# A gated recurrence with its r and z gates in PSUM banks of their own: r's newest term and the whole of z as one fp32 matmul each

## What is computed

```python
def step(h, xs):
    xzt, xrt, xht = xs
    z = jax.nn.sigmoid(xzt + h @ U_z + vz)
    r = jax.nn.sigmoid(xrt + h @ U_r + vr)
    hh = jnp.tanh(xht + r * h @ U + vh)
    h_new = (1.0 - z) * h + z * hh
    return (h_new, h_new)
```

## Time and profile before

| | |
|---|---|
| median of 3 runs | 760.3 us (759.01 to 761.73) |
| span of the profiled execution | 755.7 us; its own time is not given apart from the span |
| recurrence in the span | 203.9 to 740.8 us |
| TensorE products busy | 640.4 us (85%) |
| TensorE weight loads busy | 528.5 us (70%) |
| VectorE, ScalarE, GpSimd busy | 461.1, 324.6, 178.0 us |
| granted TensorE clock, mean | 0.956 |

### The profile page before, as it was taken

One profiled execution on the slowest core, in us unless ns is written; L12 is line 12 of the kernel. 1 busy time (PEld: TensorE's weight loads), 2 busy tenths in 40 slices (PEclk: granted clock), 3 DMA queues, 4 the chain that ended last, 5 costly groups with the idle time before them and its releaser, 6 DMA issues.

```text
span 755.7 us, 26078 instructions
## 1 busy us (share of the span) xinstructions
PE 640.4 (85%) x7909; PEld 528.5 (70%) x7909; DVE 461.1 (61%) x3362; ACT 324.6 (43%) x1253; POOL 178.0 (24%) x789
## 2 busy tenths in 40 slices
PE   5998677656788888988889898889888889999995
PEld 4445566545677877877778787778777667877774
DVE  1536344343267777777777777777767556777663
ACT  2356434434145546455555555464544222322321
POOL 1023222221033232232232332322311001111110
PEclk9999967899589999999999999999999999999997
DMA  8022222222212221222212221212210000000000
GB/s 221 9 85 76 85 88 79 92 79 79 76 40 67 74 69 65 67 71 68 71 64 65 74 64 65 74 64 67 72 62 3 2 2 2 10 6 3 4 6 8
DMA packets 43965, 43.06 MB, mean 57 GB/s; under 512 B 5500, under 2 KB 43656, under 8 KB 43784
## 3 DMA queue, kind: packets, MB, share of 16 engines
q1 hardware_dynamic: 43328, 40.75, 16.6%
q10 hardware_dynamic: 584, 1.64, 0.6%
HBM read 20.95 MB, written 21.43 MB: 56 GB/s over the span
## 4 chain that ended last, share of the span: by engine, by line
PE 54%; DVE 14%; DMA 14%; issue 9%; ACT 7%; SPq 1%; DVEq 1%; ACTq 0%; POOLq 0%; POOL 0%
DMA skew<-e_sb 13%; PE bank L622 12%; PE bank L635 12%; PE bank L423 7%; PE bank L407 6%; DVE s_sb L845 3%; ACT hh L765 3%; PE bank L440 2%; DVE g L996 2%; DVE q L988 2%; ACT oT L651 2%; PE bank L455 2%; PE bank L527 2%; PE bank L457 2%; PE bank L453 2%
## 5 line engine op out<-in xcount | busy, mean ns | idle before, releaser
L355 POOL COPY x_nat<-d 128x4 f32 (+1 forms) x256 | 53.5, 209 | 395.7 <-DVE d L1001 395.7
L635 PE MATMUL bank<-q,uc 128*128 128x54 f32 (+1 forms) x512 | 106.1, 289 | 43.3 <-DVE q L988 40.8
L635 PEld LDWEIGHTS bank<-q,uc 128*128 128x128 f32 x512 | 77.7, 190 | 90.3 <-DVE q L988 85.6
L622 PE MATMUL bank<-g,uw 128*128 128x54 f16 (+1 forms) x2560 | 119.1, 189 | 3.6 <-DVE g L996 3.6
L755 ACT ACTIVATE trz<-bank 128x8 f32<-128x8 f32 x256 | 45.5, 178 | 167.9 <-PE bank L622 167.6
L622 PEld LDWEIGHTS bank<-g,uw 128*128 128x128 bf16 x2560 | 103.6, 97 | 17.1 <-DVE g L996 7.9
L622 PE MATMUL bank<-b,uw 128*128 128x54 f16 (+1 forms) x2560 | 110.1, 188 | 0.0
L651 ACT ACTIVATE e_sb<-bank 128x132 f32<-128x132 f32 (+1 forms) x256 | 84.2, 382 | 57.6 <-DMA skew<-e_sb 55.5
L622 PEld LDWEIGHTS bank<-b,uw 128*128 128x128 bf16 x2560 | 108.1, 103 | 1.0 <-issue 0.2
L765 ACT ACTIVATE hh<-bank 128x4 f32<-128x4 f32 x256 | 44.5, 174 | 135.7 <-PE bank L635 131.3
L996 DVE TENSOR_TENSOR g<-z,hh 128x4 f16<-128x4 f32 x256 | 41.9, 164 | 97.5 <-ACT hh L765 97.5
(11 more groups left out here) (133 smaller groups left out, 1054.4 us busy)
## 6 DMA issues: line engine op xcount, KB each, us to landing
skew<-e_sb SPq DMA_DIRECT2D x128, 159.5 KB, 2.7
pos<-skew SPq DMA_DIRECT2D x128, 128.0 KB
wkv_sb<-in_L_attn_Wkv ACTq DMA_DIRECT2D x1, 1024.0 KB, 8.3
x_nat<-in_x SPq DMA_DIRECT2D x1, 512.0 KB, 4.6
wq_sb<-in_L_attn_Wq ACTq DMA_DIRECT2D x1, 512.0 KB, 5.3
wo_sb<-in_L_attn_Wo SPq DMA_DIRECT2D x1, 512.0 KB, 7.3
out<-y_out SPq DMA_DIRECT2D x8, 64.0 KB
ffn_nat<-in_L_ffn_w_gate SPq DMA_DIRECT2D x1, 256.0 KB
```

The costliest lines, as they stand in the source:

```text
L622: ins = mm(out_, uw[:, gate, use, j, :], operand, start=False, stop=True, skip_group_check=True)
L635: mm(c_cols(k, n), uc[:, :], st["q8"][:, now, 0:n], start=False, stop=True, skip_group_check=True).then_inc(c_pre, 1)
```

## The change

Each gate gets a bank of its own (`pre_cols`: bank 0 for r, 1 for z, 2 for the candidate), and r and z each get a tanh instruction. For r, the kept part is still added early from b1 and b2 (three and two bf16 products), and the new part is one fp32 product on g8 with a new fp32 matrix `u32`. z has no early part: it is one fp32 product on d8, the whole new state. g1 and g2 are gone. On VectorE q8 waits for r's tanh only; z8, b8 and b1, in this order now, wait for z's. `b2` waits for b1 as well as b8. The seed is three copies, placed behind q8, b1 and g8 of the step. The inputs of r and z stand ahead of `first_window` (`gate_inputs`, r's at k = 2 and 14, z's at k = 3 and 15) instead of in the main window; the candidate's stay there, the next period's at k = 15 instead of 14. The filler goes to bank 2.

```diff
+            def gate_inputs(i, k, last):
                 if k == 2:
                     pe.wait_ge(seed_ok, 2 * i + 2)
                     inputs(i, 1, 0)
+                if k == 3:
                     inputs(i, 1, 1)
...
+                    pe.wait_ge(b1_ok, t + 1)
+                    for j in range(3):
+                        mm(pre_cols(0, k, n), uw[:, j, :], st["b1"][:, before, 0:n], start=False, stop=True, skip_group_check=True)
+                    pe.wait_ge(b2_ok, t + 1)
+                    for j in range(2):
+                        mm(pre_cols(0, k, n), uw[:, j, :], st["b2"][:, before, 0:n], start=False, stop=True, skip_group_check=True)
+                    gate_inputs(i, k, last)
+                    first_window(i, k, groups, tiles, last)
+                    pe.wait_ge(g8_ok, t + 1)
+                    mm(pre_cols(0, k, NR), u32[:, 0, :], st["g8"][:, before, 0:NR], start=False, stop=True,
+                       skip_group_check=True).then_inc(r_pre, 1)
+                    pe.wait_ge(d8_ok, t + 1)
+                    mm(pre_cols(1, k, NZ), u32[:, 1, :], st["d8"][:, before, 0:NZ], start=False, stop=True,
+                       skip_group_check=True).then_inc(z_pre, 1)
                     main_window(i, k, groups, tiles, last)
...
-                    act.wait_ge(rz_pre, t + 1)
-                    act.activation(trz[:, now, :, :].rearrange("p g b -> p (g b)"), rz_cols(k), ACT.Tanh, scale=0.5).then_inc(trz_ok, 1)
+                    act.wait_ge(r_pre, t + 1)
+                    act.activation(trz[:, now, 0, :], pre_cols(0, k, B), ACT.Tanh, scale=0.5).then_inc(tr_ok, 1)
+                    act.wait_ge(z_pre, t + 1)
+                    act.activation(trz[:, now, 1, :], pre_cols(1, k, B), ACT.Tanh, scale=0.5).then_inc(tz_ok, 1)
...
-                    dve.wait_ge(trz_ok, t + 1)
+                    dve.wait_ge(tr_ok, t + 1)
                     dve.wait_ge(d8_ok, t + 1)
                     stt(s["q8"], tr, 1.0, d8, ALU.add, ALU.mult).then_inc(q8_ok, 1)
+                    seeds = k == 1 or (k == 9 and not last)
+                    if seeds:
+                        seed(0 if k == 9 else 1, 0)
+                    dve.wait_ge(tz_ok, t + 1)
+                    dve.tensor_scalar(s["z8"], tz, 1.0, SPLIT, ALU.add, ALU.mult).then_inc(z8_ok, 1)
+                    stt(s["b8"], tz, -1.0, d8, ALU.add, ALU.mult).then_inc(b8_ok, 1)
                     stt(s["b1"], tz, -1.0, d8, ALU.add, ALU.mult).then_inc(b1_ok, 1)
-                    stt(s["b8"], tz, -1.0, d8, ALU.add, ALU.mult).then_inc(b8_ok, 1)
-                    dve.tensor_scalar(s["z8"], tz, 1.0, SPLIT, ALU.add, ALU.mult).then_inc(z8_ok, 1)
+                    if seeds:
+                        seed(0 if k == 9 else 1, 1)
                     dve.wait_ge(b8_ok, t + 1)
+                    dve.wait_ge(b1_ok, t + 2)
                     dve.tensor_tensor(s["b2"], s["b8"], s["b1"], ALU.subtract).then_inc(b2_ok, 1)
                     dve.wait_ge(hh_ok, t + 1)
                     dve.wait_ge(z8_ok, t + 1)
-                    dve.tensor_tensor(s["g1"], s["z8"], s["hh"], ALU.mult).then_inc(g1_ok, 1)
                     dve.tensor_tensor(s["g8"], s["z8"], s["hh"], ALU.mult).then_inc(g8_ok, 1)
-                    dve.wait_ge(g8_ok, t + 1)
-                    dve.tensor_tensor(s["g2"], s["g8"], s["g1"], ALU.subtract).then_inc(g2_ok, 1)
+                    if seeds:
+                        seed(0 if k == 9 else 1, 2).then_inc(seed_ok, 1)
+                    dve.wait_ge(g8_ok, t + 2)
                     dve.wait_ge(hist_ok, t + 1)
                     stt(s["d8"], s["b8"], -0.5, s["g8"], ALU.mult, ALU.add).then_inc(d8_ok, 1)
```

More of the change, by code:

```diff
@@ L522, in inputs @@
                 x_ = x1T[:, bass.ds(i * PERIOD + block * BLOCK, BLOCK), :]
[L523 to L526, removed]
+                o_ = bank[gate][:, block * BLOCK * B:(block + 1) * BLOCK * B].rearrange("p (t b) -> p t b", b=B)
                 mm(o_, wx[:, gate, :], x_, start=False, stop=True, skip_group_check=True)
@@ L593, in main_window @@
                 if not groups[0][0]:
-                    free = bank[1 - k // BLOCK] if k not in (1, 9) else bank[3] if groups[1][0] else bank[7]
                     n = FILLER // 2 if any(s_ in TILE_MAIN for _, s_ in tiles_at(i, k, tiles)) else FILLER
-                    mm(free[:, 0:n], uw[:, 0, 0, 0, :], zeros[:, 0:n], start=(k in (1, 9)), stop=True, skip_group_check=True)
+                    mm(bank[2][:, 0:n], uw[:, 0, :], zeros[:, 0:n], start=False, stop=True, skip_group_check=True)
+                if k == 4:
+                    inputs(i, 1, 2)
+                if k == 15 and not last:
+                    inputs(i + 1, 0, 2)
+            def gate_inputs(i, k, last):
                 if k == 2:
@@ L618, in period @@
                     n = WIDE_BESIDE if groups[0][0] else WIDE
-                    def product(out_, gate, use, operand, low):
-                        for j in range(3 - low):
-                            ins = mm(out_, uw[:, gate, use, j, :], operand, start=False, stop=True, skip_group_check=True)
-                        return ins
-                    for use, name, ok in ((1, "b", (b1_ok, b2_ok)), (0, "g", (g1_ok, g2_ok))):
-                        if name == "g":
-                            first_window(i, k, groups, tiles, last)
-                        for low in range(2):
-                            pe.wait_ge(ok[low], t + 1)
-                            for gate in range(2):
-                                ins = product(rz_cols(k, gate, n), gate, use, st[f"{name}{low + 1}"][:, before, 0:n], low)
-                    ins.then_inc(rz_pre, 1)
+                    NR, NZ, NC = n, n, n
+                    pe.wait_ge(b1_ok, t + 1)
[12 more added lines that the diff above has]
+                       skip_group_check=True).then_inc(z_pre, 1)
                     main_window(i, k, groups, tiles, last)
                     pe.wait_ge(q8_ok, t + 1)
-                    mm(c_cols(k, n), uc[:, :], st["q8"][:, now, 0:n], start=False, stop=True, skip_group_check=True).then_inc(c_pre, 1)
+                    mm(pre_cols(2, k, NC), uc[:, :], st["q8"][:, now, 0:NC], start=False, stop=True, skip_group_check=True).then_inc(c_pre, 1)
             periods(pe, period)
@@ L817, in _ @@
             for n, item in enumerate(KQV):
-                if n % 2 == 1 and n // 2 < 13:
+                if n % 2 == 1 and n // 2 < 8:
                     split_u(n // 2)
@@ L973, in window @@
                     tile_stage(tau, step)
-                if k == 1 or (k == 9 and not last):
-                    seed(0 if k == 9 else 1)
             def period(i, groups, tiles, last):
```

75 lines of the change are left out of this document (35 added, 40 removed).

## The result

The changed kernel takes **810.6 us**, the median of four runs (806.99 to 817.72); the kernel before took 761.0 beside it (759.01 to 762.62). The ratio is 1.068 [1.0627, 1.0732]: 50 us slower. I had forecast 752 and faster, with 766 as the upper end.

The account below looks back on a forecast made before the run. Beside attention TensorE bounds half the steps and VectorE the others; alone mostly a latency chain. From 755.7 us, -4.1 beside attention and -3.9 alone give 747.7, plus 4.6 from span to median: 752, range 741 to 766.

Parts of the forecast that it names:

- likeliest case: Whole kernel: the summed gains beside attention and alone give 752 us; chance 0.48, own range 745 to 758.
- The clock falls: Rival: with fifteen products a step gone, TensorE drops to 1.2 GHz; 40 such steps give 766 us; chance 0.08.
- price of the moved inputs: Input products of r, z and candidate leaving the main window: +0.2 or +0.3 in some PE steps, about +0.1 alone.
- A step is 0.36 longer: Alone at 1.2 GHz: two fp32 products on the chain, each 0.457 instead of 0.275 us; 23 such steps eat the gain.
- PE steps: Eight of 16 steps beside attention, next window holding value products, TensorE never idle; forecast about +0.75 us a period.
- VectorE steps: The other eight of 16 beside attention, paced by VectorE; without g1 and g2 seven gain 0.16 each, -1.1 us a period.
- PE term: Sum over the eight PE steps of a period beside attention: about +0.75 us, plain ones +0.03 or about 0.
- cheap 0.13: Rival: r and z fp32 products cost 0.13 us each behind other work, giving 735 us; chance 0.10.
- four-pass figure of 0.09: Skill's rule for a 54-column fp32 product: 0.09 us, making PE steps 0.26 shorter; set aside for the measured 0.22.
- bare chain: Recurrence behind attention: loop of tanh, q8, candidate, hh, g8 and r, forecast at 1.78 us a step against 1.91.
- seed steps of k = 0 and 8: Alone: two seeds a period leave VectorE's path to q8, -0.37 us each, with the shorter chain.
- z's branch becomes the loop: Rival: TensorE waits for b2 behind z's tanh, z8, b8, b1, window work queued behind it; 764 us, chance 0.17.

Follow-up runs that it names:

- e12: Changed kernel, same narrow products, second-half r and z inputs moved behind the candidate's product or between b products, candidate's next input back to k = 14: 766.25 us, ratio 1.012.
- e17: e12 with 96-column fp32 products in the first two periods behind attention, and 512-column zero fillers from k = 6 of the first: 752.8 us, ratio 0.990.
- e10: Kernel before, all twenty bf16 products kept, with the change's separate banks, two tanhs and seeds behind q8, inputs placed as in e12: 757.4 us, ratio 0.998.
- e1_wide: Changed kernel with the three fp32 products of a step (r, z, candidate) 96 columns wide, zeros added, instead of 54 or 60: 779.2 us.
- e16_first_alone: e12 with 96-column fp32 products in the first period behind attention only, and 512-column zero fillers there from k = 6: 761.6 us, ratio 1.003.
- e9_mix: e1_wide with e12's input places, r and candidate narrow at k = 5 to 12 beside attention and behind the first period alone, fewer fillers: 765.8 us.

## Why the prediction was wrong

**The step that failed is the choice of the likeliest case**, a sum at full clock. The clock fell, and that took some 45 us. The rival "The clock falls" named the mechanism, but with a chance of 0.08 and a price that was too low. I argued it by the work taken away and looked for it alone, behind 585 us; it fell beside attention too, where I had not thought of it. A second step failed beside it, the price of the moved inputs: at full clock the changed kernel would still take some 765 and not 752.

- *Its price.* "A step is 0.36 longer", from two fp32 products on the chain. The seven steps of one 24 us stretch (k = 14 of one period to k = 4 of the next) are 8.2 us longer than at full clock, 1.2 each. Beside attention TensorE has every product in the loop, so all of them stretch. At 1.2 a step some 40 steps at half clock give the 45 us; I had +14 for 40 steps.
- *Waits at k = 2.* "At k = 2, 13 and 15 a moved input product costs +0.1 or takes most of a gain", which I had for the periods alone, counted the product and not the wait that moved with it; beside attention I had nothing for it. `seed_ok` comes behind the third copy, ahead of a whole window of work: +0.37 on the step beside attention, +0.7 alone (2.60 against 1.92). I had read the order of VectorE's copies and the place of the input apart from each other.
- *Beside attention, at full clock.* Forecast: PE steps +0.75, VectorE steps -1.1, together -0.37 a period. Measured in the changed kernel: +1.1 and -0.3, together +0.8. The steps k = 1, 2, 13 and 14, where the inputs stand, make the difference: r's two products fall into VectorE steps, where I had priced nothing. Without them the VectorE term holds: in e12 it is -1.1, so what leaving out g1 and g2 gives back was right.
- *The PE term is right by luck.* e12 has +0.7 there, but my +0.75 had +0.5 of input products in it, and in e12, which has most of them elsewhere, the same two steps lose 0.25. The rest comes from places where I had a gain or less of a loss: the step with the residual gained 0.05 and not 0.16, the first one with the seeds lost 0.08 and didn't gain 0.08, and a plain step, k = 4, lost 0.08 where I had 0.03. The 34.2 of e12 meets my forecast by these errors as well.
- *Prices.* r and z 0.19 each, against 0.22; neither the cheap 0.13 nor the four-pass figure of 0.09. L420 starts 0.61 behind c and not 0.47: b2 is made at q8 + 0.49 where I had 0.41, and its two products take 0.11 and not 0.05. These two errors work against each other.
- *Alone.* The bare chain is 1.77 against 1.78 forecast, and the seed steps of k = 0 and 8 gained 0.36 against 0.37. But a period with the experts takes 32.1 where 32.0 stood before and I had 0.6 less: k = 1 has +0.7 and k = 13 +0.5. That e17 is 3.7 us shorter than before there (152.2 against 155.9), and I had 3.9, is luck: its periods with the experts gain 1.3 each, the first one, with fillers and zeros, loses 0.3.
- *z's branch becomes the loop.* Alone it is refuted: the bare chain has its 1.77, so the wait for b2 does not bind. Beside attention this wait is longer than I had it (L420 at c + 0.61) and is part of what a plain PE step loses; it is small beside the clock.
- *The total.* e17_two_wide takes 752.8, and I had forecast 752. It isn't the change that I priced: its inputs stand elsewhere and it has zeros and fillers. What can be said is that fp32 gates in these places and at full clock are 1.0% faster than the kernel before, where e10, with the twenty bf16 products in the same places, is 0.2% faster.

By "TensorE: Matmul & The Clock Gate" of the Trainium skill, section on the HAM clock gate, activity releases the throttle. The rows agree in kind: zeros bring the clock back (e1_wide, 812.2 to 771.9 us of span). That a loop which is bound by TensorE in half of its steps falls to 1.2 GHz, and keeps 2.4 GHz beside attention when its input products stand elsewhere, is shown by these runs alone.

**What stays open.** Why the stretches come in every third period; whether the stop at k = 2 acts by its idle time or by moving the work around it, and what the inputs of k = 14 and 15 do, where nothing stops; why the second period alone falls in e16_first_alone while the narrow ones behind it hold in e17_two_wide. The inputs' old places in the main window were not tried with the new banks, which ScalarE reads at that time.

## What to carry to other kernels

When a change takes many small products off the busiest engine, ask first whether its clock will hold: read the granted clock of the stretches, and price the fall with every product of the loop, not those on the chain. When an instruction moves, its waits move with it: look up what raises each semaphore now, and what is queued behind the wait. And before judging such a change by its time, run it once with zero columns added, which tells the clock's part from the rest; the zeros have a price of their own, here 0.4 us a period (35.8 against 35.4).

## What the runs showed that I had not expected

- Adding work that computes nothing made a kernel faster: 96 columns instead of 54 or 60 in three products a step took the span from 812.2 to 771.9 us.
- The same products in the same number lost the clock for 24 us in every third period, or not at all beside attention in the profiled execution, by where the small input products stood (810.6 against 766.3 us).
- Executions of one kernel differ in whether the clock falls at one place: e9_mix took 753.9 us twice and 765 to 768 four times.
